# Scan layer of an eight-layer kernel: rows of C split in two parts and not three, selection taken from the identity, one POOL instruction moved

## The reference

```
x_dbl = einsum('bld,ed->ble', x, x_proj_w)
delta_r, B, C = x_dbl[..., :128], x_dbl[..., 128:144], x_dbl[..., 144:160]
delta = softplus(einsum('blr,dr->bld', delta_r, dt_proj_w) + dt_proj_b)
A = -exp(A_log)
# for every channel d and state n of 16, along the tokens t:
h[t] = exp(delta[t] * A) * h[t-1] + delta[t] * u[t] * B[t]
y[t] = sum over n of h[t] * C[t];  result y + u * D
```

## Time and profile before

| | |
|---|---|
| median of 3 runs | 1942.68 us (1942.01 to 1944.75) |
| profiled execution, its own time | 1947.12 us |
| its span | 1945.3 us |
| busy: PE, DVE, ACT, POOL | 1580.6, 1103.1, 910.6, 711.9 us |
| scan layer in the span | about 570 to 726 us |
| scan layer's loop | 610.78 to 721 us |

### The profile page before, as it was taken

The page is one execution under the profiler, slowest core; times in us unless marked ns, Lnnn a source line. Parts: engine busy times, 40 slices in busy tenths (PEclk is TensorE's granted clock), DMA queues, the critical chain, the costliest instruction groups (busy, mean ns, idle before and its releaser), DMA issues. The chain is left out here.

```text
span 1945.3 us, 27408 instructions
## 1 busy us (share of the span) xinstructions
PE 1580.6 (81%) x9258; PEld 1161.8 (60%) x9258; DVE 1103.1 (57%) x2141; ACT 910.6 (47%) x1925; POOL 711.9 (37%) x700
## 2 busy tenths in 40 slices
PE   6899789779864663837999999999999999998373
PEld 4444578668752222725776677767777677776262
DVE  4665354665458985446555555566455655554533
ACT  2365334234424323425555566555655565564342
POOL 3011260415044747046434343444343444420603
PEclk9899799888987995868999999999999999999586
DMA  3321324213324004430000000000000000000443
GB/s 76 52 50 50 110 100 126 76 50 113 125 61 174 0 10 158 144 114 14 10 17 12 6 12 17 9 9 12 12 7 12 12 9 12 7 7 3 161 141 103
DMA packets 80214, 106.57 MB, mean 55 GB/s; under 512 B 12336, under 2 KB 64176, under 8 KB 79696
## 3 DMA queue, kind: packets, MB, share of 16 engines
q1 hardware_dynamic: 73936, 88.04, 15.2%
q0 software_dynamic: 6144, 16.79, 2.7%
HBM read 70.64 MB, written 27.72 MB: 51 GB/s over the span
## 5 line engine op out<-in xcount | busy, mean ns | idle before, releaser
L1307 DVE TENSOR_SCALAR_CACHE_REDUCE gqa_scaled<-acc,gqa_neg_scale 128x128 bf16<-128x128 f32 (+7 forms) x256 | 208.9, 816 | 312.6 <-PE acc L1459 311.2
L1479 PE MATMUL aux<-gqa_probsT,gqa_v 128*128 128x512 f32 (+3 forms) x768 | 272.1, 491 | 11.2 <-DVE gqa_turned_k L1263 7.0
L1200 ACT ACTIVATE gqa_probsT<-aux 128x512 f32<-128x512 f32 (+3 forms) x384 | 174.4, 490 | 188.1 <-PE aux L1470 188.1
L1190 ACT ACTIVATE gqa_probs<-acc,gqa_bias,gqa_q_scale 128x128 f32<-128x128 f32 (+7 forms) x256 | 213.5, 834 | 46.7 <-DVE gqa_scaled L1307 40.3
L1084 POOL TENSOR_TENSOR gqa_q_high<-gqa_straight,gqa_turned_q 128x512 fp32r<-128x512 f32 x64 | 87.8, 1371 | 327.5 <-DVE gqa_turned_q L1263 327.5
L1479 PEld LDWEIGHTS aux<-gqa_probsT,gqa_v 128*128 128x128 f32 x768 | 138.2, 190 | 103.0 <-issue 62.1
L1470 PE MATMUL aux<-ident,gqa_probs 128*128 128x128 f32 x1152 | 168.9, 274 | 0.3 <-ACT gqa_probsT L1200 0.3
L1458 PE MATMUL acc<-gqa_k_high,gqa_q_high 128*128 128x512 f32 (+3 forms) x384 | 156.7, 408 | 7.2 <-DVE gqa_k_low L1291 5.7
L1458 PE MATMUL acc<-gqa_k_high,gqa_q_low 128*128 128x512 f32 (+3 forms) x384 | 133.5, 348 | 0.0
L1458 PE MATMUL acc<-gqa_k_low,gqa_q_high 128*128 128x512 f32 (+3 forms) x384 | 133.0, 346 | 0.0
L1470 PEld LDWEIGHTS aux<-ident,gqa_probs 128*128 128x128 f32 x1152 | 124.6, 141 | 0.6 <-issue 0.4
(11 more groups left out here) (417 smaller groups left out, 4284.0 us busy)
## 6 DMA issues: line engine op xcount, KB each, us to landing
f_w<-in_f_up SPq DMA_DIRECT2D x64, 256.0 KB, 2.8
f_xs<-tokens_by_slot SPq DMA_DIRECT2D x108, 128.0 KB, 2.2
outputs_by_slot<-f_y_tile SPq DMA_DIRECT2D x108, 128.0 KB, 1.7
f_w<-in_f_down SPq DMA_DIRECT2D x64, 128.0 KB, 2.9
mat_qk<-mat_high SPq DMA_DIRECT2D x64, 64.0 KB, 2.3
scan_b_all<-scan_rows SPq DMA_DIRECT2D x1, 4096.0 KB, 21.0
gqa_w_q<-in_g_wq SPq DMA_DIRECT2D x32, 128.0 KB, 2.1
gqa_wo<-in_g_wo SPq DMA_DIRECT2D x32, 128.0 KB, 2.0
```

Source lines behind the costliest of these rows:

```text
L1190: act.activation(probs_of(t, 0, t + 1), scores(t), ACT.Exp, bias=bias[:, n % 16:n % 16 + 1], scale=q_scale[:, h // 2 % 2, h % 2 * NT + t:h ...
L1200: act.activation(turned_tile(t, a, b), aux[:, chunk(n, c) % 2, 0:(b - a) * P].rearrange("p (s w) -> p s w", w=P), ACT.Copy).then_inc(chunk ...
L1307: dve.tensor_scalar(scaled[:, 0:width(t)], scores(t), neg_scale[:, h // 2 % 2, h % 2 * NT + t:h % 2 * NT + t + 1], None, ALU.mult, ALU.min ...
L1479: last = pe.matmul(weigh_bank(half)[:, first:], v[:, h // GQ % 2, s, :], moving, start=s == 0, stop=s == 4 * half + 3)
```

## The change

- `parts`, `rest` and `part32` go. The rows of C are split in two on all 128 partitions of the bank: `c_high` is the value rounded to F32R, `c_low` the remainder, also F32R.
- `spread_c` makes two accumulating matmuls for each half, with `c_high` and with `c_low`: four where there were two, in F32R and not in bf16.
- `pick` is 128x32 in F32R, copied by ACT from the first 32 columns of the identity. POOL's memsets and selections for it go.
- POOL's `w_low` waits for all eight tiles of `xn` in addition.
- DVE's second step of the split and its casts go; `add_log(1)` follows `du(0)` at once.

```diff
-        pick = sb("pick", [P, ROWS], BF16)
+        pick = sb("pick", [P, ROWS], F32R)
-        parts = sb("parts", [P, T], BF16)
-        rest = sb("rest", [ROWS, 2, T])
-        part32 = sb("part32", [ROWS, 2, T])
+        c_high = sb("c_high", [P, T], F32R)
+        c_low = sb("c_low", [P, T], F32R)
...
             pool.memset(w_in_all[:, :, P + ROWS:2 * P], 0.0).then_inc(padded, 1)
-            pool.memset(pick[:, :], 0.0).then_inc(made, 1)
             norm.gpsimd(pool)
             pool.wait_ge(w_high_ready, 1)
+            pool.wait_ge(norm.xn_ready, NT)
             pool.tensor_tensor(w_low[:, :, :], w_in_all[:, :, :], w_high[:, :, :].bitcast(F32), ALU.subtract).then_inc(w_low_ready, 1)
             pool.wait_ge(w_low_ready, 1)
-            pool.memset(parts[96:128, :], 0.0).then_inc(made, 1)
-            for q in range(3):
-                pool.wait_ge(made, q + 2)
-                pool.affine_select(out=pick[32 * q:32 * q + 32, :], in_=pick[32 * q:32 * q + 32, :],
-                                   compare_op=ALU.not_equal, fill=1.0, base=0,
-                                   pattern=[[-1, ROWS]], channel_multiplier=1).then_inc(made, 1)
-            pool.wait_ge(made, 5)
...
             act.activation(w_high[:, :, :], w_in_all[:, :, :], ACT.Copy).then_inc(w_high_ready, 1)
+            act.activation(pick[:, :], core.ident[:, 0:ROWS], ACT.Copy).then_inc(pick_ready, 1)
             norm.scalar(act)
...
                 elif m == 1:
-                    act.wait_ge(split, 2)
+                    act.wait_ge(c_low_ready, 1)
...
-            bc = two(bc_banks)[0:ROWS]
+            bc = two(bc_banks)
             relu(0)
             dve.wait_ge(bc_done, 2)
             dve.tensor_copy(b_rows[:, :], bc[0:STATE]).then_inc(rows_ready, 1)
-            dve.tensor_copy(parts[0:32, :], bc).then_inc(parts_ready, 1)
-            dve.wait_ge(parts_ready, 1)
-            dve.tensor_copy(part32[:, 0], parts[0:32, :]).then_inc(split, 1)
+            dve.tensor_copy(c_high[:, :], bc).then_inc(c_high_ready, 1)
             relu(1)
-            dve.wait_ge(split, 1)
-            dve.tensor_tensor(rest[:, 0], bc, part32[:, 0], ALU.subtract).then_inc(split, 1)
+            dve.wait_ge(c_high_ready, 1)
+            dve.tensor_tensor(c_low[:, :], bc, c_high[:, :].bitcast(F32), ALU.subtract).then_inc(c_low_ready, 1)
             add_log(0)
             dve.wait_ge(delta_ready, 1)
             dve.wait_ge(norm.xnT_ready, NT // 2)
             dve.tensor_tensor(du[:, 0], delta[:, 0], core.xnT[:, 0], ALU.mult).then_inc(du_ready, 1)
-            dve.wait_ge(split, 2)
-            dve.tensor_copy(parts[32:64, :], rest[:, 0]).then_inc(parts_ready, 1)
-            dve.wait_ge(parts_ready, 2)
-            dve.tensor_copy(part32[:, 1], parts[32:64, :]).then_inc(split, 1)
-            dve.wait_ge(split, 3)
-            dve.tensor_tensor(rest[:, 1], rest[:, 0], part32[:, 1], ALU.subtract).then_inc(split, 1)
-            dve.wait_ge(split, 4)
-            dve.tensor_copy(parts[64:96, :], rest[:, 1]).then_inc(parts_ready, 1)
             add_log(1)
...
                 for hf in range(2):
-                    last = pe.matmul(c_banks[:, hf, :], pick[:, row:row + 1].to_broadcast([P, P]),
-                                     parts[:, hf * HALF:(hf + 1) * HALF], start=True, stop=True)
+                    cols = slice(hf * HALF, (hf + 1) * HALF)
+                    chosen = pick[:, row:row + 1].to_broadcast([P, P])
+                    pe.matmul(c_banks[:, hf, :], chosen, c_high[:, cols], start=True, stop=False)
+                    last = pe.matmul(c_banks[:, hf, :], chosen, c_low[:, cols], start=False, stop=True)
                 last.then_inc(c_spread, 1)
...
-            pe.wait_ge(parts_ready, 3)
-            pe.wait_ge(made, 5)
+            pe.wait_ge(c_low_ready, 1)
+            pe.wait_ge(pick_ready, 1)
             spread_c(0)
```

More of the change, by code:

```diff
@@ L2306, in scan_layer @@
         w_low_ready = sem("w_low_ready")
-        made = sem("made")
+        pick_ready = sem("pick_ready")
         a_ready = sem("a_ready")
@@ L2314, in scan_layer @@
         b_in = [sem(f"b_in{g}") for g in range(len(GROUPS))]
-        split = sem("split")
-        parts_ready = sem("parts_ready")
+        c_high_ready = sem("c_high_ready")
+        c_low_ready = sem("c_low_ready")
         dt_done = sem("dt_done")
```

## The result

The changed kernel takes 1934.23 us (median of 6 runs, 1931.79 to 1937.95), the kernel before 1944.67 us in the runs beside it (6 runs, 1942.01 to 1947.95). The ratio is 0.9947, 95% interval 0.9933 to 0.9961: faster by 0.0053 x 1944.67 = 10.3 us, between 7.6 and 13.0. A second set of runs of the same kernel gave 0.9941 (0.9927 to 0.9954). The forecast was 1935.0 us, a gain of 7.7. The direction, the range and the places hold; the forecast gain lay at the low edge of what was measured. That the two times lie only 0.8 us apart is partly luck: the forecast counted from 1942.68 us, 2.0 us under the 1944.67 that the kernel before took in all six runs.

The account below looks back on a forecast made before the run. DVE was taken to bound the loop, with engine handovers and C's split in front of it. Gains of 1.66 and 6.98 less costs of 0.45 and 0.49 gave 7.70 us: 1942.68 to 1935.0 us, range 1932.0 to 1939.0.

Parts of the forecast that it names:

- Part 1: Normalisation: POOL's w_low waits for all xn, the last xn pair takes 0.73 us, the projection starts 1.66 us earlier.
- `low` beside the subtraction: Normalisation: POOL's subtraction beside DVE's low(1) and low(2) charged nothing; 0 to 0.8 us late if held up.
- ACT's copy of `pick`: Normalisation: the new 128x32 copy ahead of xnT_high(0), under 0.60 us, delays nothing.
- The clock in the projection: Projection: PE's clock rises the same 5 us after its start as now; 0.75 us lost or won otherwise.
- third rival: Projection and loop start: the clock rises sooner in both, 0.75 + 0.45 us more, gain 8.9 us, 1933.8 us; 20%.
- main forecast: Whole change: gain 7.70 us, 1935.0 us; 54%.
- Part 2: Between projection and loop: C split in two parts, not three; scan(1) moves from 612.98 to 606.0, 6.98 us won.
- Part 3: PE in the loop: four fp32r matmuls per spread, not two bf16; costs 0.45 us at the start, 0.49 at the end.
- Steady cost: Loop steps: nothing, PE's 2.65 us a step being covered by DVE's 3.32 us.
- At the end: Last product of the loop: waits for the spread 0.49 us longer because of two more matmuls.
- At the start: First loop steps: first spread at half clock, 0.45 us lost; nothing with an earlier rise, 1.75 with a late one.
- second rival: Loop: PE becomes the bound; 1.2 us lost, 1936.2 us, or 57 us added, 1992 us; 5% for slower.

Follow-up runs that it names:

- e1: The changed kernel without POOL's new wait for xn; ratio 0.9947 to the kernel before.
- e12: The changed kernel without POOL's new wait and with the removed POOL memset put back into a spare tile; one execution, 1937.73 us beside 1948.59.
- e2: The kernel before with only POOL's new wait for xn added; ratio 0.9988 to the kernel before.
- e6: The changed kernel with matmuls of zeros in PE's gaps of the normalisation; ratio 0.9943 to the kernel before.
- e3: The changed kernel with the removed copy back of C put in again ahead of relu(1), to a spare tile; ratio 0.9934 to the kernel before.
- e4: The changed kernel with add_log(1) moved from DVE to POOL at step 11 of the loop; ratio 0.9932 to the kernel before.
- e7: The changed kernel without the spread's matmuls on c_low, two instead of four, so C is rounded; ratio 0.9947 to the kernel before.
- e8: The changed kernel with eight matmuls in a spread, each pair made twice; ratio 1.0004 to the kernel before.
- e5: The changed kernel with 36 matmuls of zeros while PE waits for the loop's first product; ratio 0.9943 to the kernel before.

## Why the prediction was right, point by point

**Part 1, 1.66 us.** Right in size (1.66, 9.78 for 11.44), wrong in a part of its cause. I put all of 1.69 us down to the subtraction. e1 gives it 0.94 us and e12 the other 0.72 to the memset of `parts`, which I had listed among the things that "gated nothing else". For the sum it made no difference, since the change takes both away. It does for whoever makes only a part of the change: the wait alone brings all of it (e2, 1.67), and beside the removal of the memset the wait is worth 0.93 (e1 against the changed kernel). `low` beside the subtraction cost nothing, as forecast. ACT's copy of `pick` delayed nothing that shows in the 9.78.

The page "SBUF — State Buffer" of the Trainium skill, section "Who interferes with whom", says that a VectorE `tensor_scalar` can use the ports it shares with GpSimd, and that whichever instruction starts first has them to its end. The 1.67 and 2.39 us agree with that, for a POOL instruction that only writes too.

**The clock in the projection.** Forecast as unchanged, give or take 0.75. Measured 0.72 us better ("to B" 10.11 for 10.83) in the first trace, and 10.09 to 11.26 over the profiles with the same code there, e2 with the old split among them (10.23). So the delay before the rise does vary from one execution to the next, within the 0.75 us either way that the prediction allowed, and nothing shows that the 0.72 us are the change's: they are luck. In the first profile the clock rose sooner in both places, as in the third rival (gain 8.9 forecast, 8.85 measured in the layer); in the second the layer's gain is near the main forecast. At the full clock the stretch takes 8.59 (e6).

**Part 2, 6.98 us.** Measured 7.13. The missing cast back brought nothing (e3). The port went from "two casts and a subtraction, each held" to one short hold of POOL, DVE came first, and POOL set the start of the loop (e4). The small rest of 0.15 us: scan(0) came 11.29 us after the copy of B's rows where the prediction had 11.39, and scan(1) followed 2.30 us later, at the end of scan(0), where the prediction had it wait 2.35 for POOL.

**Part 3.** Steady cost nothing, as forecast (e7). The price of 0.23 a matmul held in e8, and with it the bound: at 1.72 us for the sums PE's step would pass DVE's with the seventh matmul, an estimate, as only two, four and eight were run. At the end 0.49 was forecast, the wait grew by 0.59. Of this e7 gives 0.46 to the two extra matmuls; in e7 two fp32r matmuls already cost 0.83 where two bf16 had cost 0.70. At the start 0.45 was forecast, 0.23 measured, up to 1.19 in other executions. The second rival, PE as the bound, was not true. A selection does take longer to load than in bf16, 0.19 us for 0.10 (mean of 48 loads in the windows from 620 to 700 us), as the prediction feared; but load and matmul overlap (0.23 us from start to start), also with one column repeated 128 times.

**The sum.** Forecast 7.70 for the layer, measured 8.85 and, in the second profile, 7.89: 1.66 + 0.72 + 7.13 - 0.84 = 8.67 to the last product in the first one, and 0.18 behind it. The terms off in size are the clock's (0.72 where I had 0), part 2 (7.13 for 6.98) and the two ends of the loop (0.84 where I had 0.94), and the 0.18 had no term.

**Outside the layer** the span shrank by 3.4 us more, for which the prediction had no term: 0.49 ahead of it, 3.0 from the attention layer's first statistics to the last layer's last statistics (939.2 to 936.2 us), 0.7 at the end, against 0.8 lost in the layer between. The 3.0 us lie in two places. At the start of the attention layer it is again the rise of the clock. Windows at the same distance from that layer's start, first the changed kernel, then e5:

```profile
865.98:869.98 4.00, 1.99 (x6) 1.49 (x7) 2.43 (x4) 2.25 (x4) 1.61 (x4) 0.50 0.11 35
869.98:873.98 4.00, 4.00 (x14) 3.15 (x14) 2.04 (x3) 2.58 (x4) 0.00 (x0) 0.65 0.34 100
```

```profile
867.79:871.79 4.00, 1.99 (x6) 1.49 (x7) 2.43 (x4) 2.25 (x4) 1.61 (x4) 0.50 0.11 36
871.79:875.79 4.00, 4.00 (x11) 3.03 (x11) 2.04 (x3) 2.47 (x3) 0.00 (x0) 0.50 0.36 100
```

The same code in both, 14 matmuls in one and 11 in the other. From the attention layer's first statistics to SP's first transfer of the last layer (`f_w_router`) it is 930.71 us before, 929.64 in the changed kernel and 930.64 in e5: 1.07 us won in one profile with the new split and 0.07 in another, so this part is chance.

The other 1.98 us lie at the last layer's start, where ACT and DVE wait for that transfer to land. SP's issue and ACT's first reader before, in the changed kernel and in e7:

```profile
1797.27 0.33 SPq L398 DMA_DIRECT2D f_w_router<-in_f_router  x1
...
1800.86 0.23 ACT L476 ACTIVATE f_w_router_high<-f_w_router 128x32 fp32r<-128x32 f32 x1 [8.16 <-DMA f_w_router<-in_f_router]
```

```profile
1787.62 0.33 SPq L398 DMA_DIRECT2D f_w_router<-in_f_router  x1
...
1789.23 0.23 ACT L476 ACTIVATE f_w_router_high<-f_w_router 128x32 fp32r<-128x32 f32 x1 [6.17 <-DMA f_w_router<-in_f_router]
```

```profile
1788.83 0.33 SPq L398 DMA_DIRECT2D f_w_router<-in_f_router  x1
...
1792.51 0.23 ACT L476 ACTIVATE f_w_router_high<-f_w_router 128x32 fp32r<-128x32 f32 x1 [8.25 <-DMA f_w_router<-in_f_router]
```

The reader starts 3.59 us after the issue before, 3.26 in e2, and 1.53 to 1.72 in 11 of the 12 profiles with the new split; in the twelfth, e7, it is 3.68. So the late landing also happens with the new split. Whether it happens less often there, and by what way, no run shows: two profiles of the old split are too few. The table's ratios point to more than chance: the whole kernel's gain by the ratio is 0.6 to 4.4 us above the layer's gain in one profile (both against the kernel before) in each of the 11 rows with the new split and a ratio, and 0.1 below it in e2. So some 2 to 3 us outside the layer may belong to the change. It stays open, and with it how much of the 10.3 us is the layer's 8 to 9 and how much chance.

## What to carry to other kernels

When two engines share a port, list all that both issue in the stretch, memsets too, and look at each slow instruction on its own before giving a pair's delay to one neighbour. Here a split that costs PE two matmuls more was free in the steps that DVE owned, and was paid where DVE waits for PE: at the first steps, with PE at half its clock, and at the last. Profile one kernel twice before crediting a change with a difference of two profiles: here the clock alone moved this layer by 1 us, and one transfer that landed late moved the last layer by 2. Before pricing a chain that is shortened, ask who is next: here ACT's logarithm swallowed one removed copy and POOL's first product set the new start, 0.86 us of which a moved addition gave back.

## What the runs showed of the hardware

- A POOL memset of 32x1024 bf16, which reads nothing, held a DVE `tensor_scalar` on SBUF: the pair took 2.39 us with it and 1.67 without (e12, e1; 0.73 with neither memset nor subtraction beside it).
- Matmuls of zeros raised PE's granted clock from 0.50 to 1.00 (e5, e6), and f32 transposes then took 0.66 us for four and not 1.11. The low clock cost 1.98 to 3.13 us in this layer's normalisation and projection, and 0.23 to 1.19 us at the loop's start.
- A 128x512 fp32r matmul started 0.23 us after the one before it at the full clock, its weight load of 0.19 us hidden (e8); a bf16 load took 0.10 us.
- The first transfer of the last layer had its reader start 1.53 to 1.72 us after its issue in 11 profiles and 3.26 to 3.68 us in three (before, e2, e7).
- The stretches in which the clock does not change repeated within 0.04 us between executions, while whole runs of one kernel spread over 6 us.
